# A VectorE back transposition, paired roots and a GpSimd product in the Fourier part of a Trainium2 kernel

## The reference

```python
h = layer_norm(x @ fc0_w + fc0_b, ln0_g, ln0_b)          # lifting, 32 channels
for i in range(4):
    x1 = spectral_conv(h, w1, w2)     # rfft2, mix 12 + 12 by 12 modes, irfft2
    x2 = einsum('bchw,oc->bohw', h, conv_w[i]) + conv_b[i]
    h = layer_norm(x1 + x2, ln_g[i], ln_b[i])
    if i < 3: h = gelu(h)
h = gelu(h @ fc1_w + fc1_b); h = gelu(h @ fc2_w + fc2_b); h = (h @ fc3_w + fc3_b)[..., 0]
```

## Time and profile before

| | us |
|---|---|
| median of 3 runs | 3190.63 |
| lowest, highest | 3189.6, 3193.03 |
| the profiled execution | 3195.76 |
| its span in the trace | 3194.0 |
| PE busy in the span | 2849.9 |
| DVE busy | 2238.3 |
| ACT busy | 1881.4 |
| POOL busy | 61.8 |

### The profile page before, as it was taken

The page is one execution under the profiler, slowest core; times in us unless marked ns, Lnnn a source line. Parts: engine busy times, 40 slices in busy tenths (PEclk is TensorE's granted clock), DMA queues, the critical chain, the costliest instruction groups (busy, mean ns, idle before and its releaser), DMA issues.

```text
span 3194.0 us, 80965 instructions
## 1 busy us (share of the span) xinstructions
PE 2849.9 (89%) x31600; PEld 1808.1 (57%) x31600; DVE 2238.3 (70%) x4050; ACT 1881.4 (59%) x2175; POOL 61.8 (2%) x81
## 2 busy tenths in 40 slices
PE   7888889999898999898999879999999969964994
PEld 3544556666666666666666644434443349952893
DVE  6888677888676888776888756666666643256457
ACT  6777655666555666465666537777777734422451
POOL 0000000000000000000000010000000001000000
PEclk9999999999999999999999999999999989986897
DMA  3422246644444754364744444211111000000000
GB/s 98 133 99 86 88 171 182 208 167 167 131 170 157 215 169 162 128 191 148 226 165 160 134 145 96 66 58 59 60 60 60 30 1 1 1 1 0 1 1 14
DMA packets 98349, 335.89 MB, mean 105 GB/s; under 512 B 30185, under 2 KB 62217, under 8 KB 62345
## 3 DMA queue, kind: packets, MB, share of 16 engines
q1 hardware_dynamic: 75656, 161.51, 17.0%
q10 hardware_dynamic: 18432, 134.23, 10.3%
q0 software_dynamic: 4096, 37.75, 5.4%
HBM read 179.29 MB, written 154.14 MB: 104 GB/s over the span
## 4 chain that ended last, share of the span: by engine, by line
PE 78%; DVE 11%; ACT 5%; issue 5%; DVEq 0%; SPq 0%; DMA 0%; ACTq 0%
PE pA L1285 15%; PE pA L1293 8%; PE pT L1372 7%; PE pT L1307 5%; PE pS L1315 5%; PE pD L1329 4%; PE pD L1361 4%; PE pD L1343 4%; PE pD L460 3%; PE pA L460 3%; PE pD L1257 3%; PE pA L1275 3%; PE pT L452 2%; PE pS L452 2%; DVE arena L1649 2%
## 5 line engine op out<-in xcount | busy, mean ns | idle before, releaser
L1285 PEld LDWEIGHTS pA<-conv_bd,h_in 128*128 128x128 f32 x4096 | 479.3, 192 | 107.3 <-issue 90.6
L1285 PE MATMUL pA<-conv_bd,h_in 128*128 128x128 f32 x4096 | 517.8, 280 | 6.9 <-DVE w_sb L1600 1.5
L1607 DVE TENSOR_REDUCE small<-arena 128x32 f32<-128x1056 f32 x320 | 397.5, 1242 | 170.3 <-ACT arena L1435 165.8
L1425 ACT COPY w_sb<-pA 128x1024 f32<-128x1024 f32 x256 | 259.7, 1014 | 392.3 <-PE pA L1293 343.3
L1621 DVE SCALAR_TENSOR_TENSOR w_sb<-w_sb,small 128x1024 f32<-128x1024 f32 x320 | 386.8, 1209 | 5.0
L1446 ACT ACTIVATE h_new<-pT,bet,gam 128x1024 f32<-128x1024 f32 x256 | 307.4, 1201 | 105.7 <-PE pT L1307 97.8
L1435 ACT ACTIVATE arena<-w_sb 128x1024 f32<-128x1024 f32 x320 | 339.4, 1061 | 14.7 <-DVE w_sb L1600 3.0
L1307 PEld LDWEIGHTS pT<-cst,w_sb 128*128 128x128 f32 x2048 | 225.4, 143 | 144.9 <-issue 124.4
L1307 PE MATMUL pT<-cst,w_sb 128*128 128x128 f32 x2048 | 283.2, 282 | 23.2 <-DVE w_sb L1621 23.1
L1450 ACT COPY h_rows<-pS 128x1024 f32<-128x1024 f32 x256 | 257.1, 1004 | 66.0 <-PE pS L1315 66.0
L1315 PEld LDWEIGHTS pS<-cst,h_new 128*128 128x128 f32 x2048 | 227.8, 142 | 112.3 <-issue 71.6
(11 more groups left out here) (299 smaller groups left out, 3897.1 us busy)
## 6 DMA issues: line engine op xcount, KB each, us to landing
h_scratch<-h_new ACTq DMA_DIRECT2D x128, 1024.0 KB, 4.4
h_in<-h_scratch SPq DMA_DIRECT2D x128, 1024.0 KB, 5.2
y_scratch<-w_sb POOLq DMA_DIRECT2D x32, 576.0 KB, 8.7
y_in<-y_scratch SPq DMA_DIRECT2D x512, 36.0 KB
w_sb<-in_L_tok_w1r_dram POOLq DMA_DIRECT2D x8, 576.0 KB, 7.1
w_sb<-in_L_tok_w1i_dram POOLq DMA_DIRECT2D x8, 576.0 KB, 6.9
w_sb<-in_L_tok_w2r_dram POOLq DMA_DIRECT2D x8, 576.0 KB, 8.3
w_sb<-in_L_tok_w2i_dram POOLq DMA_DIRECT2D x8, 576.0 KB, 7.5
```

The source lines that it names most:

```text
L1285: pe.matmul(pA[:, c:c + 128], h_in[:, 1024 * n + c:1024 * n + c + 128], conv_bd[:], start=(j == 0), stop=False, skip_group_check=True)
L1607: dve.reduce_sum(var[n], sq[n % 2], axis=AX).then_inc(s["summed"], 1)
```

## The change

The pixel layout is new: partitions hold one bit of x, one of the images' bits and the low 5 bits of y, and the columns the rest, so that a transposition by 32 x 32 blocks on DVE turns channels to pixels. With that:

- back is a DVE step, SBUF to SBUF; the step on PE and the copy on ACT are gone, and the store of h_new is an ACT step of its own (put).
- the back projection in acc is eight products of 256 columns in place of four of 512, fc3 sixteen in place of eight; the lifting product runs on two groups of 64 rows, and xt is a product with the identity. The constants are permuted to match.
- f1 goes by image bit in place of channel half, so f2.0 needs only f1.0; f2 and i1 use the ring s.
- rs works on two pieces (64 columns) at once in the first and mid stage; a factor of the root moves into the scale of sq.
- scale is a GpSimd product of 128 x 1024 with the root broadcast; POOL's weights, y stores and copies stand in one order with it.
- the input load is 16 DMAs per group in place of 2; the lifting weights take 34 DMAs in place of 17.
- the tower's parameters are loaded three groups later.

```diff
@@ ORDER
     "first": {
-        "PE": ("xt.0 turn.2- back.1- acc.0 back.2- turn.3- acc.1 back.3- acc.2 f1.0- turn.0 f1.1- acc.3 f2.0- back.0 "
-               "turn.1 f2.1-"),
-        "DVE": ("red.3- rs.3- scale.3- cen.0 cen.1 cen.2 red.0 rs.0 scale.0 red.1 f1.0- rs.1 f1.1- red.2 scale.1 "
-                "f2.0- rs.2 f2.1- scale.2"),
+        "PE": ("xt.0 turn.1- acc.0 turn.2- acc.1 turn.3- acc.2 f1.0- acc.3 f1.1- f2.0- f2.1- turn.0"),
+        "ACT": ("xt.0 gelu.1- acc.0 gelu.2- sq.0 acc.1 gelu.3- sq.1 put.0- put.1- acc.2 sq.2 acc.3 pack.0- sq.3 pack.1- gelu.0"),
+        "DVE": ("red.3- rs.1- cen.0 cen.1 back.0- cen.2 back.1- back.2- red.0 back.3- red.1 f1.0- rs.0 f1.1- f2.0- red.2 f2.1-"),
+        "POOL": ("scale.1- scale.2- scale.3- scale.0"),
     "mid": {
-        "PE": ("i1.0 turn.2- back.1- acc.0 i1.1 turn.3- back.2- acc.1 back.3- acc.2 f1.1- turn.0 f1.0- acc.3 f2.0- "
-               "turn.1 f2.1- back.0"),
-        "ACT": ("gelu.2- back.1- acc.0 sq.0 gelu.3- back.2- acc.1 sq.1 back.3- acc.2 sq.2 gelu.0 acc.3 sq.3 pack.0- "
-                "gelu.1 back.0 pack.1-"),
-        "DVE": ("red.3- i1.0 rs.3- scale.3- cen.0 cen.1 i1.1 red.0 rs.0 scale.0 red.1 rs.1 f1.1- scale.1 red.2 f1.0- "
-                "rs.2 f2.0- cen.2 scale.2 f2.1-"),
+        "PE": ("i1.0 turn.1- acc.0 i1.1 turn.2- acc.1 turn.3- acc.2 f1.0- acc.3 f1.1- f2.0- f2.1- turn.0"),
+        "ACT": ("gelu.1- acc.0 put.0- gelu.2- sq.0 acc.1 gelu.3- sq.1 acc.2 sq.2 acc.3 sq.3 pack.0- gelu.0 pack.1- put.1-"),
+        "DVE": ("red.3- i1.0 rs.1- cen.0 back.0- back.1- i1.1 cen.1 back.2- red.0 cen.2 back.3- red.1 f1.0- red.2 rs.0 f1.1- f2.0- f2.1-"),
+        "POOL": ("scale.1- scale.2- scale.3- scale.0"),
...
     "last": {
-        "DVE": ("scale.2- red.3- turn.2- rs.3- i1.0 scale.3- turn.3- acc.0 red.0 rs.0 acc.1 fc3.0- scale.0 turn.0 i1.1 red.1 rs.1 scale.1 acc.2 turn.1 red.2 rs.2 fc3.1- acc.3"),
+        "DVE": ("red.3- turn.2- rs.3- i1.0 turn.3- acc.0 red.0 rs.0 acc.1 fc3.0- turn.0 i1.1 red.1 rs.1 acc.2 turn.1 red.2 rs.2 fc3.1- acc.3"),
+        "POOL": ("scale.2- scale.3- scale.0 scale.1"),
@@ RING
-    "first": dict(xt="s", back="s", f1="d", f2="d"),
-    "mid": dict(i1="d", back="s", f1="d", f2="d"),
+    "first": dict(xt="s", f1="d", f2="s"),
+    "mid": dict(i1="s", f1="d", f2="s"),
@@ sync
             def load_x(g):
-                src = ins["x"].rearrange("(g b t) y x c -> g b y t (x c)", t=2, b=2)
-                for b in range(2):
-                    sp.dma_start(x_in[64 * b:64 * b + 64], src[g][b]).then_inc(s["x_loaded"], 16)
+                src = ins["x"].rearrange("(g b t) (h y) (e n r) c -> g e b t y h n (r c)", b=2, t=2, h=2, e=2, n=4)
+                for e in range(2):
+                    for b in range(2):
+                        for t in range(2):
+                            for h in range(2):
+                                q = 64 * e + 32 * b
+                                sp.dma_start(x_in[q:q + 32, t, :, 24 * h:24 * h + 24], src[g][e, b, t][:, h]).then_inc(s["x_loaded"], 16)
@@ gpsimd
+                def scale(n, g):
+                    pool.wait_ge(s["rooted"], at("rooted", ph, L, g, n + 1 if ph == "last" else n // 2 + 1))
+                    alone(pool)
+                    z = raw[n].rearrange("p (x o) -> p x o", x=32)
+                    r = rstd[n].rearrange("p (x o) -> p x o", o=1)
+                    pool.tensor_tensor(z, z, r.broadcast_to([P, 32, C]), ALU.mult).then_inc(s["normed"], 1)
...
+            def layer(ph, L, do, prepared):
+                bodies(ph, do, 1, 2)
...
+                else:
+                    mixed(L, 1)
+                    weights(prepared, 0, 0)
+                    bodies(ph, do, 2, 3)
+                    weights(prepared, 0, 1)
+                    bodies(ph, do, 3, 5)
                     y_store(L, 1)
+                    bodies(ph, do, 5, 6)
+                    weights(prepared, 1, 0)
+                    bodies(ph, do, 6, 7)
+                    weights(prepared, 1, 1)
+                    bodies(ph, do, 7, 15)
+                y_store(prepared, 0)
+                bodies(ph, do, NG - 1, NG)
+                channel_weights(prepared)
@@ tensor, acc
-                        for b in range(2):
-                            for t in range(2):
-                                rows = slice(64 * t, 64 * t + 64)
-                                mm = pe.matmul(pA[64 * b:64 * b + 64, 512 * t:512 * t + 512].rearrange("p (x o) -> p o x", o=C),
-                                               const["idft_y"][rows, 64 * b:64 * b + 64], T2_v[rows, xh, :, x0:x0 + 16],
-                                               start=False, stop=True, skip_group_check=True)
+                        for h in range(2):
+                            for e in range(2):
+                                for t in range(2):
+                                    rows, x = slice(64 * t, 64 * t + 64), x0 + 8 * e
+                                    out = pA[64 * e:64 * e + 64, 512 * t:512 * t + 512].rearrange("p (x h o) -> p h o x", h=2, o=C)
+                                    mm = pe.matmul(out[:, h], const["idft_y"][rows, 64 * h:64 * h + 64], T2_v[rows, xh, :, x:x + 8],
+                                                   start=False, stop=True, skip_group_check=True)
@@ vector
+                def back(n, g):
+                    dve.wait_ge(s["h_new_ok"], at("h_new", ph, L, g, n + 1))
+                    dve.transpose(h_rows[:, 1024 * n:1024 * n + 1024], h_new[:, 1024 * n:1024 * n + 1024]).then_inc(s["h_rows_ok"], 1)
```

More of the change, by code:

```diff
@@ L1165, in _, with body @@
-            pool.wait_ge(s["mix_a_full"], 6 * LAYERS)
-            pool.wait_ge(s["mix_b_full"], 6 * LAYERS)
-            pool.memset(spec[:, 0:at_col[0]], 0.0).then_inc(s["par_cleared"], 1)
-            pool.wait_ge(s["par_cleared"], 1)
+                    alone(pool)
+                pool.tensor_copy(conv_bd[:], conv_all[:, bass.ds(P * L, P)]).then_inc(s["conv_ready"], 1)
+            def body(order, early, late):
+                for op, n, is_late in parse(ORDER[order]["POOL"]):
+                    do = late if is_late else early
+                    if do:
+                        do[op](n)
@@ new lines, in bound, with bodies @@
+            def bound(do, g):
+                return {op: (lambda n, f=f: f(n, g)) for op, f in do.items()}
+            def bodies(ph, do, first, last):
+                if last - first == 1:
+                    body(ph, bound(do, first), bound(do, first - 1))
+                else:
+                    with pool.Fori(first, last) as b:
+                        body(ph, bound(do, b), bound(do, b - 1))
+            def layer(ph, L, do, prepared):
+                bodies(ph, do, 1, 2)
+                if ph == "first":
+                    weights(0, 0, 0)
+                    bodies(ph, do, 2, 3)
+                    weights(0, 0, 1)
+                    bodies(ph, do, 3, 4)
+                    weights(0, 1, 0)
+                    bodies(ph, do, 4, 5)
+                    weights(0, 1, 1)
+                    bodies(ph, do, 5, 5 + 10)
+                else:
+                    mixed(L, 1)
+                    weights(prepared, 0, 0)
+                    bodies(ph, do, 2, 3)
+                    weights(prepared, 0, 1)
+                    bodies(ph, do, 3, 5)
+                    y_store(L, 1)
+                    bodies(ph, do, 5, 6)
[6 more added lines that the diff above has]
+                channel_weights(prepared)
@@ new lines, in _ @@
+            make = lambda ph, L: steps(Phase(ph, L))
+            first = make("first", 0)
+            body("first", bound(first, 0), None)
+            layer("first", 0, first, 0)
+            body("mid", bound(make("mid", 0), 0), bound(first, NG - 1))
+            with pool.Fori(0, LAYERS - 2) as L:
+                here = make("mid", L)
+                layer("mid", L, here, L + 1)
+                body("mid", bound(make("mid", L + 1), 0), bound(here, NG - 1))
+            L = LAYERS - 2
+            here, last = make("mid", L), make("last", LAYERS - 1)
@@ new lines, in _ @@
+            layer("mid", L, here, L + 1)
+            body("into_last", bound(last, 0), bound(here, NG - 1))
+            bodies("last", last, 1, 2)
+            y_store(LAYERS - 1, 1)
+            bodies("last", last, 2, 3)
+            half = at_col[0] // 2
+            pool.memset(spec[:, 0:half], 0.0).then_inc(s["par_cleared"], 1)
+            bodies("last", last, 3, 4)
+            pool.memset(spec[:, half:at_col[0]], 0.0).then_inc(s["par_cleared"], 1)
+            bodies("last", last, 4, 5)
@@ L1170, in _ @@
+            pool.wait_ge(s["normed"], at("normed", "last", LAYERS - 1, 4, 2))
             pool.memset(XT[64:128, :], 0.0).then_inc(s["ones_set"], 1)
@@ L1173, in _ @@
             pool.wait_ge(s["ones_set"], 2)
+            bodies("last", last, 5, NG)
+            body("last", None, bound(last, NG - 1))
             token_pool(pool)
@@ L1486, in fin @@
```

(10 more changed lines are left out.)

207 lines of the change are left out of this document (95 added, 112 removed), and 7 rows, old and new, of the table ORDER.

## The result

The changed kernel takes 3139.64 us (median of 4 runs, 3133.11 to 3140.05) against 3190.11 of the kernel before on the same chip: ratio 0.9839, 95% interval 0.9823 to 0.9855. That is -50 where -115 was forecast; the time lies above the range. The profiled execution took 3139.2 (span 3137.6), against 3195.8.

What follows compares the result with a forecast made beforehand. It took PE to bound the mid and last stages, the first as much DVE's. Gains of 110 (mid) and 29 (first) less 10 (start) and 15 (mixes), rounded to -115, gave 3075 us, range 3035 to 3130.

Steps and rivals of the forecast that it cites:

- Stores land in 4.4 at the median, so 2 us are free.: Mid bodies: gelu.2- waits for the store of put.1-, which was expected to land in time, at no cost.
- wanted bodies later: POOL's queue: other DMAs behind its waits (weights, conv copy) are not needed soon, so no cost was added.
- the store gates gelu: Rival, mid bodies: stores landing in 7.5 delay gelu.2-, about 1.1 a body, 53 us, giving 3128; chance 0.10.
- The mid loop: Mid body: a loop through DVE, POOL, PE and ACT takes 25.3 against 27.64, gaining 2.3 a body, 110 us.
- The first body: First stage: the body's loop takes 22.1 against 24.0, gaining 29 us.
- PE has room there: First stage: PE's split lifting acc and eight xt products were taken to lie off the loop.
- Mixes: After mixes, POOL issues y stores or weights before scale.1-, making turn.2- late: 15 us added.
- Start: Kernel start: 31 more DMAs in SP's queue ahead of the first lifting product add 10 us.
- The last stage: Last stage: turn.1 moves by 0.3 yet ends before fc1.2; cost nothing, at most 5 us.
- the doubled instructions: Back projection of every acc and fc3: twice the instructions cost nothing; upper bound 33 us mid, 15 last stage.
- DVE waits for POOL: Rival, first body: cen.2 waits for a whole GpSimd product, at most 27 us, giving 3102; chance 0.25.

Runs made afterwards that it cites:

- e1: Changed kernel with put.1- issued by ScalarE right behind sq.1 in the mid layers, not at the body's end: 3085.24 us.
- e12: Changed kernel with the mid layers' first y store moved behind the third product of body 4, put.1- left at the body's end: 3115.10 us.
- e2: Changed kernel with the last layer's second y store sent before the following body's products, not after them: 3118.59 us.
- e11: Changed kernel with eight additional, unused identity transposes on TensorE ahead of f1.0- in the mid layers: 3167.22 us in one run.
- e3: Changed kernel with eight unused identity transposes filling TensorE's idle stretch ahead of f1 in the first stage: 3127.72 us.
- e5: Changed kernel with GpSimd's product scale.1- done ahead of the y stores and weights queued before it, at four places a layer: 3120.11 us.
- e7: Changed kernel with the sixteen loads of the first x issued by ScalarE instead of SP: 3134.93 us.
- e4: Changed kernel with the product by the root back on VectorE and GpSimd only waiting: 3268.68 us, ratio 1.0255 to the kernel before.

## Why the prediction was wrong

- **The steps that failed are two terms that the sum put at nothing.** The larger is put.1- at the end of ACT's order: "Stores land in 4.4 at the median, so 2 us are free." Ordinary puts do land in time. But in one body of each layer put.1- goes out 3.9 us behind the y store, takes 13.2 and holds gelu.2- for 7.48; and at the turns SP's load of the next layer's group 0, which the prediction did not list among those who wait for put.1-, waits for it up to 17.4. Together 54 (e1), of which the meeting is 22 (e12). The other is the sentence that what is queued behind POOL's waits otherwise is "wanted bodies later": the last layer's second y store is wanted by fin.0 within the body, 17 (e2).
- **The rival "the store gates gelu"** was the right mechanism in the wrong place. That its price, 53, comes near the 54 of e1 is luck: it is 1.1 us in each of 48 bodies, where three bodies and the turns lose it all. One median for all stores hid what the trace of before shows: four stores that went out 3 to 5 us behind a y store took 12 to 15 there too. The first of them, 4.0 behind the y store of the earlier trace rows, took 13.0, and the 2.3 us for which gelu waits for a store in the earlier trace rows were for this one. Its row, and the view of its tensor around it:

```profile
391.40 0.35 ACTq L1454 DMA_DIRECT2D h_scratch<-h_new  x1
```

```profile
DMA to landing us min/median/max: 13.0/13.0/13.0
```

- **The mid loop was right, and mis-sized to the good side:** 2.3 forecast, 2.8 measured, by a body of 24.8 for the 25.3 drawn. It closes at turn.2- behind POOL's product, as drawn (see e11). The product with its hand-overs takes 2.16 (592.00 to 594.16) where 2.57 was taken, red.3-, i1.0 and rs.1- take 4.02 where 4.24 was, and the rest is 0.1 longer than drawn.
- **The first body was right for the engines** (22.1 forecast, 21.6 at full clock). The term that is missing is TensorE's clock: 1.00 in the window of before, it is 0.91 in the changed one, where 1.9 us of idle stand ahead of f1.0-, and 1.00 again with this stretch filled. "PE has room there" looked at PE's share alone. e3 prices it at 6 to 14.
- **Mixes:** 15 forecast; the mechanism held, and e5 gives 14 to 20 by time and 31 in the two bodies of its trace. The weights, taken at a little over half of the y store, cost 4.4 a body against 6.0: POOL's wait for the mix, which also stands ahead of scale.1-, may be the reason, but e5 moves the wait and the issue together, so this is not shown.
- **Start:** 10 forecast, 12.7 measured: the first lifting product, shown for the changed kernel under e7, started at 14.05 before.

```profile
14.05 1.19 PE L1275 MATMUL pA<-arena 128*128 128x512 f32 x1 [7.06 <-DVE arena L1514]
```

- **The last stage** at nothing: right, 41.2 a body after 41.1. So were the doubled instructions: an acc still takes 2.90 (590.42 to 593.32, from acc.0 to i1.1).
- **"DVE waits for POOL"** happens, at a smaller price. cen.2 starts 0.75 us before a product ends and takes 1.57 in place of 0.98: 0.6 in 11 of 12 bodies, where 2.27 was allowed for; what the body loses by it no run shows by itself. The plainest row is the root step at 830.37: 0.18 elsewhere, 2.02 here, ending at 832.39, with the product on POOL (830.40 + 1.92 = 832.32). By the rule of the Trainium skill (SBUF - State Buffer, "Who interferes with whom") a two-input instruction waits until GpSimd ends; cen.2 agrees. The root step, a tensor_scalar with a single tensor input, waits as well, and the same section names tensor_scalar among the instructions that can contend with GpSimd.

The sum by terms: -136 and -36 for the bodies, +6 to 14 clock, +54 put.1-, +17 y store of the last layer, +14 to 31 mixes, +13 start: -68 to -43, where -50 is measured by the medians.

## What to carry to other kernels

An engine that only issued DMAs and now also computes puts every DMA behind the product ahead of it, and every product behind the wait ahead of a DMA: list for each who waits for it, and put first what is ready first. The landing time of a store is not a constant: look at what else is issued in the same few microseconds, and issue a store as soon as its data is there. Relief for the engine that bounds a stage pays only if its work does not turn the next engine into the bound (e4), and the clock of the relieved engine may fall (e3).

## What the runs showed of the hardware that was not expected

- Beside GpSimd's product VectorE's transpositions and reductions keep their length (1.25 and 1.21 with and without); the two-input cen.2 and the root's first step wait for its end (1.57 for 0.98, and up to 2.02 for 0.18).
- A 1 MB store issued 1 to 5 us behind the start of a y store (four parts of 576 KB) took 12 to 16 us to land in these runs, where 4 to 5 is the median; one issued 2.2 us ahead of it took 4.2 (e12).
- GpSimd's 128x1024 product with a broadcast operand took 1.92, less than half of the 4.54 of the 128x2048 one.
